# A causal attention core rebuilt on tiles of 128, 128 and 17 rows, and a quantising step moved one batch ahead

## The reference

```
h = concat(patches @ W.T, txt)
h = h + attention_0(layernorm(h))      # one head, causal
h = h + ffn_0(layernorm(h))            # quantised: act_qdq takes one maximum over ALL batches
h = h + attention_1(layernorm(h))      # 16 heads of 16, causal, rotary; heads 0-5, 6-9, 10-15 differ
h = h + ffn_1(layernorm(h))            # full attention of 16 heads, then a mixture of 8 experts
```

## Time and profile before

| | us |
|---|---|
| median of three runs | 5362.57 |
| the profiled execution | 5353.59 |
| its span | 5351.9 |
| PE busy (share of the span) | 4154.1 (78%) |
| DVE busy | 3616.3 (68%) |
| ACT busy | 2328.8 (44%) |
| POOL busy | 566.3 (11%) |

### The profile page before, as it was taken

The page is one execution under the profiler, slowest core; times in us unless marked ns, Lnnn a source line. Parts: engine busy times, 40 slices in busy tenths (PEclk is TensorE's granted clock), DMA queues, the critical chain, the costliest instruction groups (busy, mean ns, idle before and its releaser), DMA issues. The chain is left out here.

```text
span 5351.9 us, 95492 instructions
## 1 busy us (share of the span) xinstructions
PE 4154.1 (78%) x26543; PEld 2646.2 (49%) x26543; DVE 3616.3 (68%) x8340; ACT 2328.8 (44%) x4738; POOL 566.3 (11%) x905
## 2 busy tenths in 40 slices
PE   6999788700058888677778777688869999799998
PEld 5777566600035555355555555466624444355554
DVE  4555333388868888776767677477767777477777
ACT  1222233376533333266777777533336666311110
POOL 0111000000000000100000000022211111122221
PEclk9999899955579999767777787799979999899999
DMA  2222233378944444333222222277745444311110
GB/s 82 74 74 74 73 144 134 149 243 284 391 169 127 127 127 128 92 74 74 74 67 70 76 70 65 64 186 193 191 100 126 121 118 123 89 51 52 54 53 30
DMA packets 397633, 617.00 MB, mean 115 GB/s; under 512 B 49690, under 2 KB 316541, under 8 KB 397533
## 3 DMA queue, kind: packets, MB, share of 16 engines
q1 hardware_dynamic: 388284, 614.39, 39.8%
q0 software_dynamic: 9248, 1.39, 0.2%
HBM read 345.06 MB, written 269.21 MB: 115 GB/s over the span
## 5 line engine op out<-in xcount | busy, mean ns | idle before, releaser
L1222 PE MATMUL ps<-k_downT,f_o 128*91 128x256 f32 x1152 | 259.8, 385 | 459.5 <-DVE f_o L1130 459.4
L2812 PE MATMUL ps<-m_we,m_xT 128*128 128x512 f32 x1104 | 505.0, 601 | 0.0
L2143 DVE TENSOR_REDUCE e_neg<-ps 128x2 f32<-128x546 f32 x512 | 369.7, 723 | 131.7 <-PE ps L1916 122.7
L1222 PEld LDWEIGHTS ps<-k_downT,f_o 128*91 128x91 f32 x1152 | 182.8, 161 | 528.2 <-issue 461.7
L2078 ACT ACTIVATE e_probT<-ps 128x546 f32<-128x546 f32 x512 | 320.6, 627 | 229.5 <-PE ps L1922 224.9
L1493 PE MATMUL ps<-c_mask_kq,c_identb 91*91 91x91 bf16 x1536 | 322.4, 241 | 107.1 <-ACT g_probT L1607 75.0
L1495 PE MATMUL ps<-g_q,g_k 102*91 102x273 bf16 (+5 forms) x1536 | 327.1, 293 | 49.7 <-DVEq L1680 48.4
L2747 DVE SCALAR_TENSOR_TENSOR m_acc<-ps,m_weight,m_acc 128x256 f32<-128x256 f32 x552 | 257.6, 480 | 115.6 <-PE ps L2812 102.2
L2812 PEld LDWEIGHTS ps<-m_we,m_xT 128*128 128x128 f32 x1104 | 202.7, 192 | 212.5 <-issue 195.5
L587 DVE TENSOR_REDUCE b_new<-b_gu 128x1 f32<-128x1638 f32 x64 | 119.0, 1859 | 275.8 <-ACT b_gu L651 275.8
L1493 PEld LDWEIGHTS ps<-c_mask_kq,c_identb 91*91 91x91 bf16 x1536 | 215.1, 150 | 177.0 <-ACT g_probT L1607 129.5
(11 more groups left out here) (324 smaller groups left out, 9613.6 us busy)
## 6 DMA issues: line engine op xcount, KB each, us to landing
s_gate<-b_gu SPq DMA_DIRECT2D x32, 819.0 KB, 4.6
s_up<-b_gu SPq DMA_DIRECT2D x32, 819.0 KB, 6.0
c_g<-s_gate SPq DMA_DIRECT2D x32, 819.0 KB, 7.1
s_gated<-c_g SPq DMA_DIRECT2D x32, 819.0 KB, 8.6
d_g<-s_gated SPq DMA_DIRECT2D x32, 819.0 KB, 10.9
d_u<-s_up SPq DMA_DIRECT2D x32, 819.0 KB, 11.0
s_o<-d_o SPq DMA_DIRECT2D x32, 819.0 KB
f_o<-s_o SPq DMA_DIRECT2D x32, 819.0 KB, 4.8
```

What stands on the lines that cost most here:

```text
L1222: last = nc.tensor.matmul(ps[0:R, t // 2, (t % 2) * D:(t % 2 + 1) * D], o[:, u, k, t * R:(t + 1) * R], downT[:, k, :], start=(k == 0), sto ...
L2143: nc.vector.tensor_reduce(neg[:, u, g // 2, :, 4 * (g % 2) + a], ps[:, bank:bank + 2, 0:T], AX.X, ALU.max, negate=True).then_inc(S["looked ...
L2812: last = nc.tensor.matmul(ps[0:R, EBANK[m % 4], :], xT[:, u, k, t * R:(t + 1) * R], we[:, k, 2 * p:2 * p + 2, :].rearrange("p e d -> p (e ...
```

## The change

1. `phase_b` becomes a pipeline: x of batch n+1 is rounded and scaled between the gate half and the up half of batch n, into a buffer of its own.
2. The causal core is written anew as `attention_causal`. Tiles are 128, 128 and 17 tokens. A unit is one head's two whole tiles in one bank (a look 128 + 256 columns, a product by key 273 + 145), so the 17-row tiles of four heads ride in a unit of their own (looks) or in the fourth head's bank (by key). One ring of six banks serves 33 units a body, main units (MAIN) and looks (PRE) in a fixed mixture. One mask matmul covers both tiles of a unit. The four hyperbolic heads lie side by side in one buffer of 1698 columns, and all passes but one go over them together. Their shifts lie in a small tensor `qs`, multiplied by a row block of ones.
3. The heads are reordered on the host to plain (0 to 5), normalised (6 to 11), hyperbolic (12 to 15); `phase_f1` follows, and takes the normalised heads' scale of 4 into the norm (`guard`), so that no exponential has a scale. V is stored by token.
4. `attention_full` contracts over 99 rows instead of 128 in the main products, so the buffers q, probT and probR need no clearing, only three rows of k are set to one, and the first loads wait for nothing.

The core of the diff:

```
 # phase_b
+        xq = sb("xq", [128, 2, CT, T])
+ SP:   pipeline(sp, NB, ((store(0, gate_dram), 0), (next_x, 1), (store(1, up_dram), 0)))
+ ACT:  pipeline(act, NB, ((copy(0), 0), (quantise, 1), (copy(1), 0)))
+ DVE:  pipeline(dve, NB, ((largest(0, "g", amax_gate), 0), (scale_x, 1), (largest(1, "u", amax_up), 0)))
+ PE:   pipeline(pe, NB, ((both, 0),))
 # phase_f1
-                sp.dma_start(v_dram[batch_of(n)], vp[:, u].rearrange("p t h w -> p (t h w)"))
+                sp.dma_start(v_dram[batch_of(n)].rearrange("(t p) w -> p t w", p=R), vp[:, u].rearrange("p t h w -> p t (h w)"))
-                nc.gpsimd.tensor_scalar(ss[:, u, :, 4:NSCALED], ss[:, u, :, 4:NSCALED], 1e-24, None, ALU.max)
+                nc.gpsimd.tensor_scalar(ss[:, u, :, 0:6], ss[:, u, :, 0:6], 1e-24, 0.25, ALU.max, ALU.mult)
 # attention_core goes, attention_causal comes
+        UNITS = [(MAIN, 0), (PRE, 0), (PRE, 1), (MAIN, 1), (PRE, 2), (PRE, 3), (MAIN, 2), (PRE, 4), (PRE, 5),
+                 (MAIN, 3), (PRE, 6), (PRE, 7), (PRE, 8),
+                 (MAIN, 4), (PRE, 9), (MAIN, 5), (PRE, 10), (MAIN, 6), (PRE, 11), (MAIN, 7),
+                 (MAIN, 8), (PRE, 12), (MAIN, 9), (PRE, 13), (MAIN, 10), (PRE, 14), (MAIN, 11), (PRE, 15), (PRE, 16),
+                 (MAIN, 12), (MAIN, 13), (MAIN, 14), (MAIN, 15)]
+        RING = 6          # unit p waits until the bank of unit p - 6 is free
+            def look(bank, of_q, of_k):
+                mask_two(bank, mask_look, 256)
+                over(bank, 0, 128, of_q[:, 0:128], of_k[:, 0:128])
+                return over(bank, 128, 256, of_q[:, 128:256], of_k[:, 0:256])
+            def by_key(bank, of_k, of_q, masked_):
+                over(bank, 0, T, of_k[:, 0:128], of_q[:, 0:T], masked_)
+                return over(bank, T, T - 128, of_k[:, 128:256], of_q[:, 128:T], masked_)
+ PE body: emit((MAIN, 0), (PRE, 0), (PRE, 1)); turn_back(post, pu, 2); products(0, 0)
+          emit((MAIN, 1), (PRE, 2), (PRE, 3)); products(0, 1); emit((MAIN, 2), (PRE, 4), (PRE, 5)); products(0, 2)
+          emit((MAIN, 3), (PRE, 6), (PRE, 7), (PRE, 8)); wait laid[u][0]; emit((MAIN, 4), (PRE, 9)); turn_back(post, pu, 3)
+          products(1, 0); emit((MAIN, 5), (PRE, 10)); products(1, 1); turn(now, u, 1); emit((MAIN, 6), (PRE, 11))
+          products(1, 2); emit((MAIN, 7)); emit((MAIN, 8), (PRE, 12)); turn_back(now, u, 0); products(2, 0)
+          emit((MAIN, 9), (PRE, 13)); products(2, 1); emit((MAIN, 10), (PRE, 14)); products(2, 2)
+          emit((MAIN, 11), (PRE, 15), (PRE, 16)); wait laid[u][1]; emit((MAIN, 12)); turn_back(now, u, 1); products(3, 0)
+          emit((MAIN, 13)); products(3, 1); turn(then, tu, 0); emit((MAIN, 14)); products(3, 2); emit((MAIN, 15))
+ ACT body: exponential 0, 1; scores(now); exponential 2; copy_sum(post, 3); exponential 3, 4, 5; first_part(now, 1)
+          log_of_square(then); exponential 6; copy_sum(now, 0); exponential 7; root_of_square(then); exponential 8, 9
+          second_part(now, 1); exponential 10; distance(then); copy_sum(now, 1); exponential 11
+          log_of_distance(then, 0), (then, 1); exponential_hyp 0, 1; first_part(then, 0)
+          log_of_distance(then, 2), (then, 3), (then, 4); exponential_hyp 2; second_part(then, 0); copy_sum(now, 2); exponential_hyp 3
+ DVE body: tops 0, raw 0; divide(post, 2); tops 1, raw 1, ... raw 3; top_scores; negate_tops(now)
+          clamp(then); largest 0; square(then); divide(post, 3); largest 1; remainder(now, 1); largest 2, 3; divide(now, 0)
+          largest_rest 0; add_root(then); largest 4; third_part(now, 1); largest 5; largest_rest 1; join_largest
+          add_shift 0; divide(now, 1); add_shift 1; remainder(then, 0); add_shift 2; third_part(then, 0); add_shift 3
+ POOL body: spread_hyp(now); lay(now, 1) [three DMAs to qs]; spread_plain(then); lay(then, 0) [three DMAs to q]
+            def clamp(n, u):   nc.vector.tensor_scalar(hw[:, u], hw[:, u], -1.0, 2.0 ** -23, ALU.add, ALU.max)
+            def square(n, u):  nc.vector.scalar_tensor_tensor(out=hu[:], in0=hw[:, u], scalar=2.0, in1=hw[:, u], op0=ALU.add, op1=ALU.mult)
+            def add_root(n, u): nc.vector.tensor_tensor(hw[:, u], hw[:, u], hu[:], ALU.add)
 # attention_full
-            sp.wait_ge(ones_set, 1)
-            sp.wait_ge(cleared, 5)
+            sp.wait_ge(cleared, 2)      # now behind the loads of q and k, ahead of those of V
-            nc.vector.memset(q[96:128], 0.0)      # and probT, probR
-            nc.gpsimd.memset(k[96:128], 1.0)
+            nc.gpsimd.memset(k[DEEP:DEEPER, 1], 1.0)
+            nc.vector.memset(k[DEEP:DEEPER, 0], 1.0)
```

More of the change, by code:

```diff
@@ new lines, in lay, with body @@
+            def lay(n, u, p):
+                pool.wait_ge(S["lo"].sem, S["lo"].at(n, p + 1))
+                pool.sem_inc(passed, 1)
+                for part in range(PARTS):
+                    to = qs[part:part + 1, u, :, :] if p else q[DEEP + part:DEEP + part + 1, u, 0:NS, 0:T]
+                    pool.dma_start(to, shift[0:NHYP if p else NS, u, p, part, :]).then_inc(laid[u][p], 16)
+            def body(i, b, here, earlier, posts):
+                _, (now, u, _), (then, tu, _) = sides(i, b)
+                if here[MAIN]:
+                    spread_hyp(now, u)
+                    lay(now, u, 1)
+                if here[PRE]:
+                    spread_plain(then, tu)
+                    lay(then, tu, 0)
@@ L1483, in _ @@
+            program(pool, body)
         @block.tensor
         def _(pe):
-            for x in ("look", "s", "turn", "pv", "back"):
+            for x in ("look", "turn", "s", "pv", "back"):
                 S[x].give(pe)
-            if n_hyp:
-                pe.wait_ge(ready, 7)
-            def tile(bank, col, w, mask, stationary, moving, col_of_mask):
-                out_ = ps[0:R, bank, col:col + w]
-                if mask is not None:
-                    nc.tensor.matmul(ps[0:R, bank, col + col_of_mask:col + col_of_mask + R], c["identb"][0:R, 0:R],
-                                     c[mask][0:R, 0:R], start=True, stop=False, skip_group_check=True)
-                return nc.tensor.matmul(out_, stationary, moving, start=mask is None, stop=True,
-                                        skip_group_check=mask is not None)
@@ L1583, in _, with halves, mask_two @@
-            program(pe, step)
+            pe.wait_ge(masked, 16)
+            def halves(bank, first, second):
+                flat = ps[:].rearrange("p b c -> p (b c)")[:, bank * 512 + first:bank * 512 + first + 2 * (second - first)]
+                return flat.rearrange("p (s w) -> p s w", s=2)[:, :, 0:128]
+            def mask_two(bank, mask, second):
+                nc.tensor.matmul(halves(bank, 0, second), c["identb"][:], mask[:], start=True, stop=False,
+                                 skip_group_check=True)
@@ new lines, in mask_rest, with over @@
+            def mask_rest(bank, mask, col):
+                nc.tensor.matmul(ps[:, bank, col:col + REST], c["identb"][:], mask[:], start=True, stop=False,
+                                 skip_group_check=True)
+            def over(bank, col, w, stationary, moving, masked_=True, rows=slice(0, 128), **tile):
+                return nc.tensor.matmul(ps[rows, bank, col:col + w], stationary, moving, start=not masked_, stop=True,
+                                        skip_group_check=masked_, **tile)
@@ new lines, in turn @@
+            def turn(n, u, p):
+                pe.wait_ge(S["spread"].sem, S["spread"].at(n, 3 if p else 2))
+                pe.wait_ge(S["out"].sem, S["out"].at(n, 0) if p else S["out"].at((n[0], n[1] - 1), 2))
+                count = NHYP if p else NS
+                for t in range(2):
+                    nc.tensor.transpose(ps[0:count, TURNED, t * 128:(t + 1) * 128],
+                                        neg_h[:, u, t, :] if p else neg[:, u, t, :], c["ident"][:])
+                nc.tensor.matmul(ps[0:count, TURNED, WHOLE:T], spread_h[:, u] if p else spread_s[:, u],
+                                 stacked[:], start=True, stop=True).then_inc(S["turn"].sem, 1)
```

1140 lines of the change are left out of this document (694 added, 446 removed).

## The result

The changed kernel takes 5275.87 us (median of four runs, 5268.62 to 5286.47) against 5359.44 us for the kernel before: a ratio of 0.9848, 95% interval 0.9824 to 0.9872, or 84 us less. The forecast was 5165 us and the range ended at 5262. phase_b and the full core gave what was forecast, and the causal core became longer. The profiled execution took 5268.62 us, its span 5266.9.

A forecast was written before the change was run, and what follows sets the result against it. TensorE was taken to bound phase_b and the full core, a chain of steps handed between three engines the causal core. 5353.6 - 84.7 - 87 - 20 = 5162, plus a third of 9 us: 5165 us, range 5045 to 5262.

The forecast's parts named there:

- phase_b: In phase_b, quantising a batch ahead lets TensorE run without a gap: 355.7 us, 84.7 less.
- R4: Rival on phase_b: quantising ahead does not do what it says, phase_b gains nothing, total 5249 us; chance 0.06.
- The full core's start: Start of the full core: loads wait for nothing and less is cleared, so 20 us less, 21 at most.
- The core: Causal core: 33 us a body and 27 of fill make 1083 us instead of 1170, so 87 less.
- (a): Core, third_part(1) to add_shift(0): VectorE idle 3.2 us a body while POOL's DMAs bring the hyperbolic shifts.
- Work: Core, busy time a body: VectorE 22.7 us, ScalarE 21.3, TensorE 16 at full level or 32 at half.
- (b): End of a core body: remainder(0) and third_part(0) wait for ScalarE, 2.7 us, or 3.9 with TensorE at half level.
- (d): Start of a core body: TensorE's first product waits for the last exponential, 0.5 us, or 2.6 at half level.
- (c): Middle of a core body: turn_back waits for copy_sum(0) behind log_of_square, 1.1 us, or 3.6 at half level.
- The level: TensorE's granted clock in the core: half of the time at each level, between 0.6 and 0.8.
- R1: Rival: TensorE at half level all through, 36.0 us a body, the core gains nothing, total 5258 us; chance 0.20.
- R3: Rival: long passes stop the shared ring of six banks in turn, 41 us a body, total 5418 us; chance 0.06.

The follow-up runs named there:

- e5: The kernel before with the new phase_b alone, all other stages as before: 5272.56 us, ratio 0.9833 to the kernel before.
- e1: Changed kernel with SyncE's load of q and k of heads 0 to 7 started later, behind the hyperbolic shifts: 5176.21 us, ratio 0.9687.
- e8: Changed kernel with 96 matmuls of no use a body on TensorE, ahead of its wait for the shifts: 5255.36 us, ratio 0.9809.
- e3: Changed kernel with VectorE's divide(3) of the batch before moved ahead of largest(0) and square: 5198.73 us, ratio 0.9720.
- e9: Changed kernel with later load, earlier third part, division, exponentials 6, 7 and copy_sum(0), plus 26 useless matmuls before the shift wait: 4977.20 us, ratio 0.9302.
- e7: Changed kernel with 55 matmuls of no use a body on TensorE, ahead of its wait for the shifts: 5263.18 us, ratio 0.9824.

## Why the prediction was wrong, by its own steps

**phase_b: right.** First to last matmul takes 616.64 to 973.01, 356.4 us; 355.7 was forecast. After the one slow half that was counted, the halves follow each other at 5.53 us, as in the earlier trace rows:

```profile
616.64 7.93 PE L692 MATMUL ps<-b_xq,k_gateT 128*128 128x273 f32 x24 [16.30 <-DVE b_xq L667]
624.41 5.69 PE L692 MATMUL ps<-b_xq,k_upT 128*128 128x273 f32 x24
629.94 5.70 PE L692 MATMUL ps<-b_xq,k_gateT 128*128 128x273 f32 x24
```

R4 is out, and e5 shows the gain by itself (5359.91 to 5272.56, 87 us).

**The full core's start: right.** From phase_g1's last store to the first matmul it was 36.8 us (3888.8 to 3925.58) and is 14.0:

```profile
3848.51 1.09 PE L2247 MATMUL ps<-e_k,e_q 96*128 96x273 bf16 x4 [16.10 <-POOL e_block_mask L2205]
```

The stage as a whole, last store to last store, went from 724.0 to 703.0: -21.0, forecast -20. The other small terms lay in their bounds: phase_f1 +2.3, the core's own start 4.8 us shorter. Stages that the change doesn't touch moved by -3.6 (phase_c and phase_d), +4.8 (phase_g1) and -9.7 us (phase_g3); that was not followed up.

**The core: wrong by 118 us.** First matmul (2184.00) to last store (3385.3) is 1201.3, not 1083: 32 bodies of 36.45 instead of 33 make 110 of it, the fill 8. By the prediction's own sign (a body over 36 us) (a) or the clock was misjudged; it was (a).
- Work: VectorE's prices were right (`reduce` of 384 columns 0.55, `raw` 0.65, square and add_root 1.92, clamp 1.05), but neighbours overlap by up to 0.1 us: in the body from 2802.55 to 2838.71 durations of 22.7 us keep VectorE busy for 20.1.
- Wait (a) is the term that failed: 3.2 us forecast, 8.2 measured on VectorE (6.84 and 1.23 in the body shown). The prediction took the 4.0 us from third part to matmul out of the earlier trace rows as a property of the DMA. It was that of a stretch in which the last load of q and k had been issued 5 us before, and in which the DMA share, with a load of V (2808.91) and a store (2812.09), was 0.79 and then 0.23, where it is 1.2 now:

```profile
2806.59 1.31 SPq L1416 DMA_DIRECT2D g_k<-s_parts  x3
```

```profile
2813.00:2814.00 1.00, 0.74 (x11) 0.55 (x9) 0.44 (x1) 0.08 (x1) 0.49 (x1) 1.00 0.79 218
2814.00:2815.00 1.00, 0.22 (x2) 0.06 (x2) 0.81 (x4) 0.00 (x0) 0.00 (x0) 1.00 0.23 68
```

In the new order the load of heads 0 to 7 waits for the twelfth product by key (MAIN 11), the last one before TensorE stops for the shifts, so load and shifts start close together (1.9 us apart in the body shown). The prediction has three POOL DMAs in this step and nothing of what SyncE starts beside them. e1 gives 3.1 us a body back, of the 3.4 that were missing.

- The second part of the miss in (a): VectorE of e1 still waits 39.2 us there in nine bodies (2700 to 3000 us), 4.4 a body. Its first `add_shift` waits 3.12 us, as forecast; the second waits 1.23, for MAIN 13 behind products and transposes. The prediction names these ("TensorE's products and transposes queue too") and puts them at nothing. e8 shows 0.8 us of the 1.23 to be the level.
- Errors that cancel: the 33 us were 22.7 of work and 10.3 of waits; here it is 20.2 and 16.7, so work priced 2.5 us too high hides part of the miss. That e1's body (33.4) comes out near 33 is luck to that extent: it is 19.8 of work and 13.3 of waits (119.7 us in nine bodies). Nor is its 5176 us within 11 of the forecast on equal terms, since the kernel before ran at 5346 beside it; by the ratio it is 5192.
- Waits (b) and (d) came out near their prices: 2.5 us for the parts of the shift at the end of a body (9.4 of the 15.5 us, and the 10.9, by 8.06; 2.7 to 3.9 forecast for (b)), 1.7 at `tops` (0.5 to 2.6).
- Wait (c) is 3.5 us on VectorE (the other 6.1 of the 15.5, 13.7 and 8.7), at the upper end of its 1.1 to 3.6. e3 shows that it is on the path to (a): an edit there that leaves TensorE's wait for the shifts as it was still takes 2.6 us off a body.
- The level: 0.66 to 0.68, inside the 0.6 to 0.8 forecast. R1 gave nearly the right time (5258) and the right body (36.0) by the wrong mechanism: e8 holds the level up behind the shifts and gains 0.8 us. The rule of the Trainium skill named there, "TensorE: Matmul & The Clock Gate", section "A second HAM failure mode: psum-queue depth-cycling", agrees with the traces as far as the swing goes (0.50 and 1.00 in one body, with six banks too). Holding the level up was worth 0.8 us a body in e8 and, once the waits had shrunk, 1.6 in e9 (0.9397 to 0.9302, 51 us, by 32); what e3 owes to the level was not separated.
- R3's ring did not stop the passes: TensorE's large waits are those for the shift DMA (62.4 us) and at the turn (22.4), not for a bank.
- A slip in the sums: 28 us a body would be 32 x 28 + 27 = 923 us, so -247 and not -240. Nothing hangs on it.

## What to carry to other kernels

When a short DMA is put on the path, look up which bulk loads are released by the same event or just before it, and price the landing from a stretch of the trace with such a load in flight; here one number in the load's wait was worth 86 us. Give the chain that ends in such a DMA the first place in every queue that it passes: moving two small steps ahead of long passes was worth 218 us, more than the whole change. A clock at half level is a cause only if holding it up moves the end, which fillers in the idle stretch can test.

## What the runs showed of the hardware

- A 2.1 KB DMA that POOL issues 1.9 us behind SyncE's loads landed in 5.1 us, and in 1.5 us with a DMA share near 0 beside it (medians, changed kernel and e1).
- In the changed kernel TensorE stood 2.76 us, worked 1.5 us at 1.00 and was then at 0.50 for 3.4 us; in e3 it stood 2.09 us and went on at 1.00; in e7, 4.7 us of fillers at 1.00 and then 3.25 us idle ended at 0.50 (one body each).
- Neighbouring VectorE instructions on small tiles start 0.08 to 0.13 us apart with durations of 0.15 to 0.21 us (the four from 2809.97 on in the changed kernel), so their durations can't be added to a time.
